# Eight buffers for gathered tokens in place of six, and a gather lead of six duos in place of four

## The reference

```
x = x + L0(group_norm(x))        # linear attention: q, k, v = xf @ w_qkv; q, k layer-normed per head (8 x 32);
                                 # out = q @ (k^T v) / n
t = t + L1(layer_norm(t))        # softmax attention over the 1024 tokens, 8 heads of 32, then w_agg and b_agg
t = t + FFN(layer_norm(t))       # routed experts
# FFN:
gate_logits = x @ gate_weight                    # (b, n, 8 experts)
gates = sinkhorn(gate_logits)                    # 8 rounds of column and row normalisation
vals, idx = top_k(gates^T, n // 8)               # each expert takes 128 tokens of each batch
outputs = (x[idx] @ experts[e]) * vals
result = zeros.at[idx].set(outputs)              # scattered back to the tokens' rows
```

## Time and profile before

| | us |
|---|---|
| median of three runs | 1470.48 |
| lowest, highest | 1467.41, 1474.88 |
| profiled execution, its own time | 1466.12 |
| span of the profile (first to last instruction) | 1463.7 |
| mean granted TensorE clock | 0.933 |

### The profile page before, as it was taken

The page is one execution under the profiler, slowest core; times in us unless marked ns, Lnnn a source line. Parts: engine busy times, 40 slices in busy tenths (PEclk is TensorE's granted clock), DMA queues, the critical chain, the costliest instruction groups (busy, mean ns, idle before and its releaser), DMA issues.

```text
span 1463.7 us, 28099 instructions
## 1 busy us (share of the span) xinstructions
PE 1303.8 (89%) x10413; PEld 868.8 (59%) x10413; DVE 1006.3 (69%) x2149; ACT 832.0 (57%) x1236; POOL 592.4 (40%) x1132
## 2 busy tenths in 40 slices
PE   5789889999999999999999999999998999785634
PEld 3655565657665766576657666656565657563423
DVE  3536764868476847684768576968888668599770
ACT  2355656677667766776677667566666674341100
POOL 1132530355135513551455145412464057655543
PEclk8889989999999999999999999999999999898655
DMA  2043003600460036003600360027000573334421
GB/s 79 1 137 81 1 30 80 181 16 10 102 180 16 21 92 179 16 30 88 174 16 30 88 173 16 12 74 189 33 1 1 135 231 113 123 116 137 120 81 60
DMA packets 69391, 119.36 MB, mean 82 GB/s; under 512 B 13057, under 2 KB 49154, under 8 KB 69250
## 3 DMA queue, kind: packets, MB, share of 16 engines
q1 hardware_dynamic: 58242, 90.49, 23.1%
q0 software_dynamic: 11008, 27.02, 6.1%
HBM read 29.12 MB, written 33.55 MB: 43 GB/s over the span
## 4 chain that ended last, share of the span: by engine, by line
PE 59%; DVE 23%; issue 6%; POOL 5%; ACT 4%; another core or an unknown queue 1%; DMA 1%; ACTq 0%; POOLq 0%; DVEq 0%
PE shared L930 29%; PE scores L886 11%; PE acc L908 10%; DVE prob_sum L1657 6%; PE acc L905 3%; ACT probs L1191 2%; PE shared L925 2%; DVE acc_sb L1631 2%; DVE bn L1328 2%; DVE work L1567 2%; DVE best_i L1565 2%; DVE best L1563 2%; DVE resid L1334 1%; PE acc L918 1%; DVE bn_x L1432 1%
## 5 line engine op out<-in xcount | busy, mean ns | idle before, releaser
L1191 ACT ACTIVATE probs<-scores 128x1024 f32<-128x1024 f32 x512 | 514.0, 1022 | 192.4 <-DVE prob_sum L1657 102.8
L886 PE MATMUL scores<-query_stack,key_stack 96*128 96x256 f32 x2048 | 347.5, 310 | 26.7 <-ACT probs L1191 25.9
L886 PEld LDWEIGHTS scores<-query_stack,key_stack 96*128 96x128 f32 x2048 | 277.2, 192 | 105.8 <-ACT probs L1191 55.5
L1657 DVE TENSOR_TENSOR prob_sum<-prob_sum,probs 128x512 f32<-128x512 f32 x512 | 339.0, 723 | 0.2
L908 PE MATMUL acc<-probs,v_all 128*32 128x256 f32 x4096 | 292.1, 392 | 5.7 <-issue 5.1
L1223 POOL TENSOR_TENSOR attn_T<-acc_sb 128x256 f32<-128x256 f32 x56 | 41.9, 748 | 409.8 <-DVE acc_sb L1631 407.0
L930 PE MATMUL shared<-w_sb,chan 128*128 128x512 f32 (+1 forms) x512 | 187.5, 503 | 5.9 <-DVE chan L1466 5.9
L908 PEld LDWEIGHTS acc<-probs,v_all 128*32 128x32 f32 x4096 | 115.4, 111 | 120.9 <-issue 44.9
L930 PEld LDWEIGHTS shared<-w_sb,chan 128*128 128x128 f32 x512 | 92.5, 193 | 68.4 <-issue 63.3
L1522 DVE TENSOR_TENSOR lo<-shared,hi 128x512 fp32r<-128x512 f32 x64 | 43.3, 684 | 128.0 <-ACT hi L1149 128.0
L930 PE MATMUL shared<-chan,w1T 128*128 128x512 f32 x256 | 122.7, 614 | 2.5 <-ACT chan L1112 2.4
(11 more groups left out here) (223 smaller groups left out, 1892.8 us busy)
## 6 DMA issues: line engine op xcount, KB each, us to landing
query_stack<-hi SPq DMA_DIRECT2D x120, 128.0 KB, 2.5
key_stack<-hi SPq DMA_DIRECT2D x120, 128.0 KB, 2.5
x_sb<-in_x_dram SPq DMA_DIRECT2D x8, 1024.0 KB, 5.6
out_dram<-resid SPq DMA_DIRECT2D x16, 512.0 KB
tokens_scratch<-resid SPq DMA_DIRECT2D x16, 512.0 KB
tokens_scratch<-rows SPq DMA_DIRECT2D x16, 512.0 KB
key_stack<-lo SPq DMA_DIRECT2D x60, 128.0 KB, 2.5
query_stack<-lo SPq DMA_DIRECT2D x60, 128.0 KB, 2.5
```

What stands on the lines that cost most here:

```text
L886: last = pe.matmul(score_ps[u % 2][:, QB * r:QB * (r + 1)], key_stack[stack, HG * g + r, P * kt:P * (kt + 1)], query_stack[stack, HG * g + ...
L1191: act.activation(probs[:, u % PROBS, :], score_ps[u % 2][:, :], ACT.Exp, scale=DH ** -0.5) \
L1657: dve.tensor_tensor(total[:, part], probs[:, (u - 1) % PROBS, part] if kt == 1 else total[:, part], probs[:, u % PROBS, part], ALU.add).th ...
```

## The change

`PICKED` goes from 6 to 8: `hi[:, 2, :]` and `hi[:, 3, :]` become two more buffers, between `hi[:, 1, :]` and the one in `v_all`. `LOOKAHEAD` goes from 4 to 6. Group 0's first six picks get a stretch of their own, slots 9.0 to 11.25 of batch 7's segment, and the other steps of the first 80 go over 11.25 to 31. The wait for the copies out of `hi` moves to the first duo that uses it (d = 4), with one more wait: that the second head group's keys and queries are copied out of `hi[:, 2:4, :]`.

```diff
-PICKED = 6
-LOOKAHEAD = 4
+PICKED = 8
+LOOKAHEAD = 6
...
     picked += [m.rearrange("p (j n) -> p j n", j=TILES)
-               for m in (hi[:, 1, :], v_all[:, G, :, :].rearrange("p t n -> p (t n)"))]
+               for m in (hi[:, 1, :], hi[:, 2, :], hi[:, 3, :], v_all[:, G, :, :].rearrange("p t n -> p (t n)"))]
...
-            7: [(11.25, 31, routing.experts(0)[:80]), *spaced(routing, 1, 15.25, 1.3),
+            7: [(9.0, 11.25, routing.experts(0)[:LOOKAHEAD]), (11.25, 31, routing.experts(0)[LOOKAHEAD:80]), *spaced(routing, 1, 15.25, 1.3),
                 (25.0, PAIRS, routing.selection(1)[:34])],
...
-                    if d == PICKED - 2:
+                    if d == PICKED - 4:
                         await_hi_free(pool)
+                        await_count(pool, "group_copied1", STACK_DMAS * all_attends)
                     if d == PICKED - 1:
                         await_count(pool, "v_copied1", 16 * all_attends)
```

## The result

| | before | changed |
|---|---|---|
| median of 20 runs of each, side by side, us | 1472.4 | 1482.9 |
| lowest, highest, us | 1465.2, 1477.2 | 1468.1, 1484.8 |
| ratio of comparable runs, 95% interval | | 1.0061 [1.0046, 1.0076] |
| span of the profiled execution, us | 1463.7 | 1475.0 |

The changed kernel is slower by 0.6%, some 9 us by the ratio and 10.5 by the two medians. The forecast was +3.0 us, and its range reached to 1480.5; the median of 1482.9 lies outside it. Three of the 20 changed times lie at 1468 to 1471 and sixteen at 1482 to 1485; the profiled one is in between. What separates the two clusters stays open.

What follows compares the result with a forecast made beforehand. PE paces 1190 to 1290, DVE is full from about 1290, and a gather chain ends the tail. Terms +3.4 + 1.0 - 0.6 - 0.6 - 0.2 = +3.0 us on a median of 1470.48 gave 1473.5 us, range 1461.5 to 1480.5.

Steps and rivals of the forecast that it cites:

- The first gather isn't earlier: Picks from slot 9: still behind POOL's transfer of reciprocals, first gather at about 1196.5 as before, gain 0.
- The waits at duos 7 and 23: PE's waits for gathers, 0.58 and up to 3.47 us, both go: -0.6 us for duo 7, 0 for duo 23.
- The scatters of group 2: End of the tail: last eight scatters still about 3 us apart; two fewer gathers ahead of them give -0.2 us.
- Group 1 in the tail, -0.6 us: Last group's ranking starts 1.5 us sooner, less expert 24's scaling of 0.88 on DVE: -0.6 us, bounds 0 and -1.5.
- Six duos ahead ... Cost 0; if the cover fails, up to 3 us: Start: 12 gathers in a row on POOL delay slot 13's transfer some 5 us, wanted only about 10 us later.
- rival A: Standstills at 1246 to 1248 and 1268 to 1276 come from the short lead and go: -10 us, 1460.5; chance 0.18.
- +3.4 for turn 0's wait: Duo 0's turn moves to slot 11, PE waits 4.5 us in place of 1.03; bounds 0 and +4.5.
- +1.0 for the clock: After turn 0's wait PE's clock stays at half for 2 us more; bounds 0 and +3.
- Nothing absorbs it: At turn 0's wait: DVE and ACT were as full as PE before it, so the +3.4 us stays.
- estimate with a transfer of 2.6 us: Turn 0's wait by the skill page's transfer time: gather 0.9 us sooner, +2.5 less the 1.03 saved before it.
- B: Turn 0's wait spreads as engines restart one after another, two more slots cost 3 us each: +9, 1479.5; chance 0.2.
- a clock of 0.50 beyond 1212: Behind duo 0, half clock for 10 us and more: the deciding sign that turn 0's wait spreads.

Runs made afterwards that it cites:

- the long run in the tail alone: The ramp with all six picks at once for groups 1 and 2, so 14 gathers in a row in the tail only; ratio 1.0055 to the kernel before.
- the ramp: Changed kernel with four picks at first, one extra after turns 1 and 2, and the old places of the steps; ratio 1.0012 to the kernel before.
- The earlier turn alone: Kernel before with its first four picks over slots 9.0 to 11.25, the rest over 11.25 to 31, six buffers, lead of four; ratio 1.0001.
- the half rows: Changed kernel, and the kernel before, with gathered rows of 1 KB in place of 2 KB; ratios 1.0049 and 0.9980 to the full kernel before.

## Why the prediction was wrong

**Right.** The first gather isn't earlier. Turn 0 waits 4.5 us in slot 11 (4.51). The waits at duos 7 and 23 are gone: of waits for `chan` two are left in place of four (4.5 us at turn 0 and 4.9 at group 2's first turn). The scatters of group 2 stay 3.0 us apart. In the tail only turn 25 stands before the ranking. The clock after turn 0's wait is at the lower level, 0.54 over 1200 to 1206.

**The step that failed: "Group 1 in the tail, -0.6 us", and with it "Six duos ahead ... Cost 0; if the cover fails, up to 3 us".** I asked of the longer run only what is queued behind it on POOL: one transfer with 10 us of slack. I took the DMAs of the run as harmless to the engines that wait for none of them. In the tail I worked out rightly that PE's transposes come directly behind DVE's input, 1.6 us sooner, and took for granted that ACT would see them 0.7 us later: 6.9 us in fact, on the path. The term of -0.6 measured +5.4 in the profile (60.8 to 66.2 us between the lists of the two groups). Some 1.4 of it is a second mistake: DVE's wait for expert 24's product, 1.98 us ahead of the ranking before, doesn't go with the new order but comes back inside the ranking. On the chip, a lead of four in the tail gave 0.4% or 5.7 us back, and the long run in the tail alone costs 6.3 us more than the ramp. At the start the run of 12 holds PE's work too and made slot 15 late by 12.6 us against a forecast of 4.4; but that this costs anything at the end isn't shown (lead of four in the tail 1.0022, ramp 1.0012, intervals overlapping).

The profile before had the clue. Among PE makes turn 1 at 1204.66, and ACT's copy of it came 5.2 us later; I never looked at who received PE's work. I also read the earlier trace rows, engines standing with no gather awaited, as something that a longer lead might cure (rival A). ACT and DVE stand there for PE work that its rows show as done, among gathers and scatters.

**The term that was right and cost nothing: +3.4 for turn 0's wait; the term that didn't come: +1.0 for the clock.** The earlier turn alone has the full wait and a ratio of 1.0001. The clock was at the lower level for about 6 us behind the wait, 1200 to 1206, and back at 1.00 over 1206 to 1212: no longer than the 6 us of the earlier trace rows. "Nothing absorbs it" was wrong twice. DVE and ACT weren't as full as PE: the stage of the earlier trace rows has them busy 9.46 and 13.06 us of 20, and DVE was idle for the 4.18 us up to 1202.62, from 2.5 us before PE stood. And between slot 15 and slot 25 DVE has 21 us of idle time; of the 12.6 us of slot 15, 3.1 were left at the ranking of group 1. (The prediction's estimate with a transfer of 2.6 us has a slip: 4.5 less 0.9 less 1.03 is already the +2.5, from which the 1.03 isn't taken again.)

**The rivals.** B took its loss to be turn 0's wait that spreads, with the clock at 0.50 beyond 1212; the size fits (+9), the mechanism doesn't: the wait alone costs nothing. Its sign, a clock of 0.50 beyond 1212, was there in part (1.00 over 1206 to 1212, 0.54 over 1212 to 1216), but behind the hold and not behind the wait. A is not what happened to the time, though both of its standstills are shorter in the changed profile: DVE's longest idle times between 1230 and 1280 are 3.96 and 3.02 us, before 10.51 and 6.30. That the forecast's "slower" came true is luck: the terms that made it +3.0 (turn 0's wait and the clock) cost nothing, and the loss came from a term that was down as a gain.

**What stays open.** Which mechanism lets a run of indirect DMAs keep PE's results from the others. The rows show that PE goes on issuing meanwhile, so its own instructions reach it. In the 7 us of the tail's hold, the instruction queues moved nothing; the trace has the software queue alone:

```profile
DMA packets 432, 1.38 MB, mean 198 GB/s; under 512 B 94, under 2 KB 94, under 8 KB 432
## 3 DMA queue, kind: packets, MB, share of 16 engines
q0 software_dynamic: 432, 1.38, 66.9%
```

So a late fetch of instructions isn't it either. Whether PE's matmuls end late or only the news of their end is late can't be told from its rows: as the page says, their ends are modelled. The Trainium skill, page "Perfetto Trace Analysis", section "Tensor Engine Instruction (MATMUL, LD_WEIGHTS)", agrees: the profiler's end is an estimate, and the semaphore is updated only once PSUM has acknowledged all bytes. No run here separates the two. The Trainium skill, page "DMA: Bandwidth & Descriptors", section "SWDGE vs HWDGE vs iDMA", says that GpSimd writes the descriptors of such DMAs into rings in SBUF; that would be a cost by number and not by bytes, as the half rows show, but no run here tests it. Nor is it known why some of PE's results inside a run come out at once and others don't. A gap of some 0.2% between the changed kernel with a lead of four in the tail (1.0022) and the kernel before is not explained by any single hold either.

## What to carry to other kernels

A longer lead is not free where nothing waits for the data: picks that are issued at once form a run, and in a long run of gathers on GpSimd engines that have no part in it can get PE's results late. Let the lead grow by one extra pick at a time, and keep the runs clear of the moment at which a full engine waits for a short result of another. Judge a moved step by when its receiver gets it, not by when its own engine makes it. And ask what paces the stretch behind a delay before adding the delay to the sum: here a wait of 4.5 us on the busiest engine cost nothing, and 5.4 us in the tail, ahead of an engine that is full from there on, came out at the end.

## What the runs showed of the hardware

- Beside 9 to 14 indirect gathers back to back (0.95 us each, 0.30 between) ACT got some of PE's transposes 2.1 to 9.2 us behind their start, and others, made in the first part of the same runs, at once (1.1 us). When PE made them 1.6 us or more behind the start of the last gather, after runs of 5 or 10, it was 0.7 to 1.3 us. Gathers and scatters mixed do the same: 6.9 us at 1242.11 in the kernel before.
- Half the bytes don't lift the hold: with 14 gathers in the tail and a DMA share of 0.35 in place of 0.67 ACT is 3.9 us late, against 3.9 to 6.9 us in the four kernels with whole rows.
- In the dense stretch of slots 15 to 25, 13 indirect scatters fewer were worth 13.0 us of DVE's idle time there and 18.5 us in all, 1.4 us each; 6.8 us of arithmetic less on POOL were worth 0.2% in all (by the interval 0.03 to 0.36).
